# Latent attention of a two-layer decoder: softmax sums formed in all rows of a head, and inverted there

## What is computed

```python
k = jnp.concatenate([k_p, k_r], axis=-1)
q = jnp.concatenate([q_p, q_r], axis=-1)
scores = jnp.einsum('bqhd,bkhd->bhqk', q, k) * scale
scores = jnp.where(causal[None, None], scores, jnp.finfo(scores.dtype).min)
probs = jax.nn.softmax(scores, axis=-1)
out = jnp.einsum('bhqk,bkhd->bqhd', probs, v).reshape(b, s, H)
return out @ o_w
```

## Time and profile before

| | us |
|---|---|
| median of 3 runs | 2243.73 (2242.27 to 2243.81) |
| the profiled execution's own time | 2242.4 |
| its span | 2240.7 |
| PE busy | 2155.5 (96%) |
| PE weight loads busy | 1796.3 (80%) |
| DVE busy | 1315.1 (59%) |
| ACT busy | 1083.3 (48%) |
| POOL busy | 674.5 (30%) |

### The profile page before, as it was taken

One profiled execution on the slowest core, in us unless ns is written; L12 is line 12 of the kernel. 1 busy time (PEld: TensorE's weight loads), 2 busy tenths in 40 slices (PEclk: granted clock), 3 DMA queues, 4 the chain that ended last, 5 costly groups with the idle time before them and its releaser, 6 DMA issues. The chain is left out here.

```text
span 2240.7 us, 43433 instructions
## 1 busy us (share of the span) xinstructions
PE 2155.5 (96%) x18048; PEld 1796.3 (80%) x18048; DVE 1315.1 (59%) x2315; ACT 1083.3 (48%) x1919; POOL 674.5 (30%) x684
## 2 busy tenths in 40 slices
PE   7998899899999999999999999999899999999996
PEld 5766666454589999999999999999777877899996
DVE  7776676689854445444544454444555455767774
ACT  5676533578744444333433343433455554325553
POOL 4111110356412221111111111211354544135663
PEclk9999999999999999999999999999999999999998
DMA  7444302100033232321223123221000000258996
GB/s 282 151 148 140 95 6 114 57 1 1 29 132 123 76 113 95 113 76 64 87 95 113 57 95 120 70 73 57 25 2 2 2 2 30 85 188 265 272 280 105
DMA packets 46931, 215.32 MB, mean 96 GB/s; under 512 B 6160, under 2 KB 6160, under 8 KB 32400
## 3 DMA queue, kind: packets, MB, share of 16 engines
q1 hardware_dynamic: 29968, 139.13, 17.3%
q0 software_dynamic: 16768, 73.41, 11.4%
HBM read 169.00 MB, written 43.52 MB: 95 GB/s over the span
## 5 line engine op out<-in xcount | busy, mean ns | idle before, releaser
L343 POOL TENSOR_TENSOR c_prob<-c_prob,c_inv_mass 128x512 f32<-128x512 f32 x128 | 130.4, 1037 | 353.2 <-DVE c_inv_mass L335 353.2
L325 ACT ACTIVATE c_prob<-abc_banks,c_neg_peak 128x256 f32<-128x256 f32 x256 | 117.7, 472 | 177.6 <-DVE c_neg_peak L317 177.6
L50 PE MATMUL abc_banks<-bc_xt,bc_wq_hi 128*128 128x256 f32 x512 | 147.7, 288 | 0.0
L50 PE MATMUL abc_banks<-c_ctx,c_wk_hi 128*128 128x256 f32 x512 | 146.6, 286 | 0.0
L51 PE MATMUL abc_banks<-bc_xt,bc_wq_hi 128*128 128x256 f32 x512 | 144.9, 283 | 0.0
L52 PE MATMUL abc_banks<-bc_xt,bc_wq_lo 128*128 128x256 f32 x512 | 144.8, 283 | 0.0
L51 PE MATMUL abc_banks<-c_ctx,c_wk_hi 128*128 128x256 f32 x512 | 143.7, 281 | 0.0
L52 PE MATMUL abc_banks<-c_ctx,c_wk_lo 128*128 128x256 f32 x512 | 143.7, 281 | 0.0
L238 PE MATMUL abc_banks<-ab_wq,b_xqt 128*128 128x512 bf16 x512 | 118.7, 383 | 4.2 <-DVE b_h L209 2.2
L2196 DVE TENSOR_TENSOR c_v_lo<-abc_banks,c_v_hi 128x512 fp32r<-128x512 f32 x64 | 44.2, 691 | 133.1 <-ACT c_v_hi L2112 133.1
L1932 POOL DMA_DIRECT2D c_ctx<-kept_scratch x24 | 13.2, 550 | 347.0 <-PE abc_banks L52 347.0
(11 more groups left out here) (590 smaller groups left out, 7223.4 us busy)
## 6 DMA issues: line engine op xcount, KB each, us to landing
x_res<-b_w SPq DMA_DIRECT2D x48, 512.0 KB, 4.7
bc_xt<-kept_scratch POOLq DMA_DIRECT2D x24, 1024.0 KB, 5.1
c_ctx<-kept_scratch POOLq DMA_DIRECT2D x24, 1024.0 KB, 5.2
e_raw<-e_w SPq DMA_DIRECT2D x15, 1536.0 KB
bc_raw<-c_w SPq DMA_DIRECT2D x16, 1024.0 KB, 4.9
h_res<-e_w SPq DMA_DIRECT2D x7, 1536.0 KB
kept_scratch<-bc_xt SPq DMA_DIRECT2D x8, 1024.0 KB, 3.8
kept_scratch<-c_ctx SPq DMA_DIRECT2D x8, 1024.0 KB, 4.0
```

What stands on the lines that cost most here:

```text
L50: pe.matmul(out, lhs[0], rhs[1], start=first, stop=False)
L325: ins = act.activation(self.prob[:, u % 2, j, :], self.s_ps[:, j, :], ACT.Exp, bias=self.neg_peak[:, u % 2, j:j + 1], accum_out=self.mass[ ...
L343: pool.tensor_tensor(part, part, self.inv_mass[:, u % 2, js].unsqueeze(2).to_broadcast([P, 2, SEQ]), ALU.mult).then_inc(self.prob_done, 1)
```

## The change

The sums are formed with a 128x32 matrix of ones, and each group r writes its own 256 columns, so that all 32 rows of a head hold the sum of that head. VectorE takes the reciprocal of all 128x512 into `inv_mass` in SBUF, which has twice the columns, and the divide reads it there. `inverses`, its four products an image and the ring's places n0 and n1 go. ScalarE's `output_high` waits for the new semaphore `divided` instead of the freed bank. GpSimd fills `ones` before the stage begins, and PE and the mask wait for it.

```diff
--- before.py
+++ after.py
@@ -2378,8 +2378,8 @@
         qt_hi, qt_lo = sb("qt_hi", [P, C, SEQ], F32R), sb("qt_lo", [P, C, SEQ], F32R)
         kt_hi, kt_lo = sb("kt_hi", [P, C, SEQ], F32R), sb("kt_lo", [P, C, SEQ], F32R)
         o_hi, o_lo = sb("o_hi", [P, C, SEQ], F32R), sb("o_lo", [P, C, SEQ], F32R)
-        o_f, inv_mass = sb("o_f", [P, 2, SEQ]), sb("inv_mass", [P, SEQ])
-        pick, share, spread_f = picks.pick, picks.share, picks.spread
+        o_f, inv_mass = sb("o_f", [P, 2, SEQ]), sb("inv_mass", [P, 2, SEQ])
+        pick, ones = picks.pick, sb("ones", [P, HD])
         neg_peak = sb("neg_peak", [P, TB, P])
         peak_t = sb("peak_t", [P, SEQ], F32R)
         s_ps = ctx.enter_context(nc.psum_tensor("d_s_ps", [P, 4, 512], F32))
@@ -2409,7 +2409,7 @@
         s_ready, peak_done, st_ready, exp_done, cut_done, w_ready = (
             sem(n) for n in ("s_ready", "peak_done", "st_ready", "exp_done", "cut_done", "w_ready"))
         o_raw_done, o_hi_done, o_lo_done, squared = (sem(n) for n in ("o_raw_done", "o_hi_done", "o_lo_done", "squared"))
-        gain_done = sem("gain_done")
+        gain_done, divided = sem("gain_done"), sem("divided")
         shared_in, small_in, shared_hi_done = sem("shared_in"), sem("small_in"), [sem(f"shared_hi_done{k}") for k in range(2)]
         UP = 2 * (late.raw.shape[1] // 3)
         block = ctx.enter_context(nc.Block())
@@ -2420,8 +2420,8 @@
 
         TURNS = range(-1, BATCH)
         PLACES = (("lq", 1), ("lk", 1), ("mt", 0), ("q0", 1), ("q1", 1), ("k0", 1), ("k1", 1), ("m0", 0), ("v0", 1),
-                  ("qt0", 1), ("qt1", 1), ("n0", 0),
-                  ("kt0", 1), ("kt1", 1), ("m1", 0), ("xt0", 2), ("xt1", 2), ("n1", 0), ("v1", 1), ("o0", 0), ("o1", 0))
+                  ("qt0", 1), ("qt1", 1),
+                  ("kt0", 1), ("kt1", 1), ("m1", 0), ("xt0", 2), ("xt1", 2), ("v1", 1), ("o0", 0), ("o1", 0))
         use_of = {}
         for i in TURNS:
             for name, ahead in PLACES:
@@ -2513,7 +2513,8 @@
 
             pool.memset(mask_f[:, :], 0.0).then_inc(blanked, 1)
             pool.memset(neg_peak[:, :, :], 0.0).then_inc(blanked, 1)
-            pool.wait_ge(blanked, 2)
+            pool.memset(ones[:, :], 1.0).then_inc(blanked, 1)
+            pool.wait_ge(blanked, 3)
             pool.affine_select(out=mask_f[:, :], in_=mask_f[:, :], compare_op=ALU.is_ge, fill=-1e30, base=0,
                                pattern=[[-1, P]], channel_multiplier=1).then_inc(masked, 1)
             pool.wait_ge(rope_in, 16)
@@ -2678,16 +2679,8 @@
                     n = C * i + 2 * h + r
                     for t in range(TB):
                         for j in range(4):
-                            mm = pe.matmul(bank[HD * j:HD * (j + 1), t * P:SEQ], share[:, r, :], prob[:, n % PROBS, j, t * SEQ:SEQ + t * P],
-                                           start=r == 0 and t == 0, stop=r == 1 and t == TB - 1)
-                mm.then_inc(ring_ready, 1)
-
-            def inverses(i, h):
-
-                await_free(pe, f"m{h}", i)
-                bank = claim(f"n{h}", i)
-                for r in range(2):
-                    mm = pe.matmul(bank[:, r * SEQ:(r + 1) * SEQ], spread_f[:, r, :], inv_mass[:, :], start=True, stop=True)
+                            mm = pe.matmul(bank[HD * j:HD * (j + 1), r * SEQ + t * P:(r + 1) * SEQ], ones[:, :],
+                                           prob[:, n % PROBS, j, t * SEQ:SEQ + t * P], start=t == 0, stop=t == TB - 1)
                 mm.then_inc(ring_ready, 1)
 
             def outputs(i, t, half):
@@ -2700,7 +2693,7 @@
                     mm.then_inc(ring_ready, 1)
 
             pe.wait_ge(begun, 1)
-            pe.wait_ge(blanked, 2)
+            pe.wait_ge(blanked, 3)
             for i in TURNS:
                 now, nxt, after = here(i), here(i + 1), here(i + 2)
                 if nxt and i > 0:
@@ -2735,8 +2728,6 @@
                 if nxt:
                     turn_queries(i + 1, 0)
                     turn_queries(i + 1, 1)
-                if now:
-                    inverses(i, 0)
                 if nxt:
                     turn_keys(i + 1, 0)
                     turn_keys(i + 1, 1)
@@ -2757,7 +2748,6 @@
                     turn_inputs(1, 1)
                     keep_busy(pe, o_ps[:, :, :].rearrange("p h q -> p (h q)"), parts["v_u"][0][:, 0:P], parts["v_u"][0], 3)
                 if now:
-                    inverses(i, 1)
                     if i == 0:
                         pe.wait_ge(w_lo_done[OUT], 1)
                         pe.wait_ge(w_lo_done[REST], 1)
@@ -2856,7 +2846,7 @@
             def output_high(i, h):
                 if h == 0 and i > 0:
                     await_ready(act, "o1", i - 1)
-                await_free(act, f"n{h}", i)
+                act.wait_ge(divided, 2 * i + h + 1)
                 act.activation(o_hi[:, 2 * h:2 * h + 2, :], o_f[:, :, :], ACT.Copy).then_inc(o_hi_done, 1)
 
             def square(i, t):
@@ -2973,14 +2963,13 @@
             def invert(i, h):
                 await_ready(dve, f"m{h}", i)
                 if 2 * i + h > 0:
-                    await_ready(dve, f"n{1 - h}", i - 1 + h)
-                dve.reciprocal(inv_mass[:, :], bank_of(f"m{h}", i)[:, 0:SEQ]).then_inc(free_of(f"m{h}", i), 1)
+                    dve.wait_ge(divided, 2 * i + h)
+                dve.reciprocal(inv_mass[:, :, :], bank_of(f"m{h}", i).rearrange("p (r q) -> p r q", r=2)).then_inc(free_of(f"m{h}", i), 1)
 
             def divide(i, h):
-                await_ready(dve, f"n{h}", i)
+                await_free(dve, f"m{h}", i)
                 dve.wait_ge(o_raw_done, 2 * i + h + 1)
-                dve.tensor_tensor(o_f[:, :, :], o_f[:, :, :], bank_of(f"n{h}", i).rearrange("p (r q) -> p r q", r=2),
-                                  ALU.mult).then_inc(free_of(f"n{h}", i), 1)
+                dve.tensor_tensor(o_f[:, :, :], o_f[:, :, :], inv_mass[:, :, :], ALU.mult).then_inc(divided, 1)
 
             def add_to_y(i, t):
                 await_ready(dve, f"o{t}", i)
```

## The result

| us | before | after |
|---|---|---|
| time, median of 8 runs each | 2243.86 (2242.27 to 2249.56) | 2252.34 (2250.47 to 2255.6) |
| the profiled execution's own time | 2242.4 | 2251.46 |
| its span | 2240.7 | 2249.7 |
| PE busy | 2155.5 | 2147.8 |
| DVE busy | 1315.1 | 1341.0 |

The account below looks back on a forecast made before the run. PE was taken as bounding, but held at scores 1 by VectorE's peak behind the second reciprocal. Turns 4.4, last turn 1.0, start 0.1 and end -0.3 gave +5.2 us on the median 2243.73: 2248.9 us, range 2245.2 to 2252.5.

Parts of the forecast that it names:

- the sum: Whole kernel: 4.4 (six turns) + 1.0 (last turn) + 0.1 (stage start) - 0.3 (last image) = +5.2 us.
- list of signs: Wrong if the reciprocal is under 2.6 us, images are no further apart, or the granted clock is below 1.00 within the stage.
- Reciprocal: VectorE's reciprocal, 256 to 512 columns: 1752 to 3352 ns, 1.60 us more, sixteen times.
- First half: Middle image: the query turn waits for the sums' bank, delaying VectorE's chain 0.13 us; PE's saved 1.28 us come to nothing.
- Second half: Middle image: the longer reciprocal delays the peak of scores 0, so scores 1 start 0.73 us later; six turns, 4.4 us.
- Last turn: Image 6 to 7: no input turns ahead, peak close behind the reciprocal; scores 1 at 1878.73 against 1877.69, +1.0 us.
- Rival 2: New PE idle stretches drop the clock to 1.2 GHz, some 1.5 us each turn: +10 more, 2259; chance 0.06.
- End: Last image: divide no longer waits for a slow spreading product; between -1.0 and +0.35 us, taken as -0.3.
- a sentence outside the sum: Last image: the divide's two SBUF operands and GpSimd's selects exclude each other, losing up to 0.3 us more.
- PE's busy time: PE's total busy time was to fall by 16 us or so, as spreading products go.
- Rival 1: Faster, since PE's products count; needs a reciprocal below 2.6 us: -3.5, or -15 without bank waits; chance 0.07.
- rival 3: Partly absorbed: no query-turn wait, earlier peak, or -1.0 usual at the end; +1 to +4, about 2246.5; chance 0.3.

Follow-up runs that it names:

- e5: The changed kernel with six unread products on PE ahead of scores 1 in the turn from image 6 to 7: 2250.75 us, 1.0027 of before.
- e2: The kernel before with each 256-column reciprocal made twice, spreading products kept: 2261.22 us, 1.0093 of before.
- e1: The changed kernel with reciprocals of 256 columns, the first group's inverses serving both groups: 2240.6 us, 0.999 of before.
- e3: The change made for half 0 of the heads only, half 1 as in the kernel before: 2251.61 us, 1.0038 of before.
- e4: The change made for half 1 of the heads only, half 0 as in the kernel before: 2250.38 us, 1.0023 of before.
- e7: The changed kernel with the second reciprocal split around the peak of scores 0, keys' parts ahead of the divide, inputs copied earlier: 2241.01 us, 0.9975 of before.
- e10: The change for half 0 only, half 1 as before, with the keys' parts ahead of the divide: 2240.43 us, 0.9974 of before.
- e9: The kernel before with only the keys' parts moved ahead of the divide, spreading products and n0 kept: 2254.81 us, 1.0046 of before.
- e8: The changed kernel with the keys' parts ahead of the divide and inputs copied earlier, reciprocal whole: 2243.88 us, 0.9991 of before.

## Why the prediction was right

The time came out at 2252.34 against 2248.9, just inside the range of 2245.2 to 2252.5. The mechanism of the turns was right. That the number fell inside was in part luck: the ends that the sum gives itself, +3.6 to +7.5 us, reach only to 2251.2, the 1.6 us that the clock cost had no term in the sum, and the medians lie 2.4 us further apart than the stage explains. By its own list of signs a granted clock below 1.00 within the stage would have made it wrong, and there was one, in the last turn. Step by step:

- **Reciprocal.** 3354 ns for a forecast 3352. The slope between the two widths of the earlier trace rows, 6.25 ns a column, held. By the estimate from the repeat count of 8 in the Trainium skill ("VectorE: DVE Perf Modes", "First, the fixed hardware budget") it would have been 4.3 us. No run agrees with that.
- **First half.** The second query turn started 0.15 after the end of the reciprocal (1722.82 against 1722.67), as forecast, the second low part was 0.15 late, the second reciprocal started 8.54 us after the first instead of 8.40: +0.14 for 0.13. PE stopped at kt1 and the input turns, 0.33 and 0.56, forecast 0.4 and 0.6.
- **Second half.** Scores 1 start 5.07 after the second reciprocal where it was 4.55: +0.52 for 0.60. The timeline of PE:

```profile
1727.48 1.23 PE L2560 MATMUL d_ring<-ident,d_a 128*128 128x128 f32 x8 [0.56 <-DVE d_kt_lo L2953]
...
1732.92 0.39 PE L2635 MATMUL d_s_ps<-d_kt_lo,d_qt_hi 32*128 32x256 f32 x4 [1.30 <-DVE d_neg_peak L2961]
```

  The forecast took 1.83 us for both reductions from the earlier trace rows. Back to back with the reciprocal they took 1731.11 to 1732.87, 1.76 (the first 0.63, not 0.69). So a turn lost 0.66 and not 0.73: 3.9 instead of 4.4.
- **Last turn.** +1.0 was forecast, +2.54 came. This is the step that was wrong: by order it is 0.94, as e5 shows, and the sum had no term for the 1.6 us of the clock there. Rival 2 named the mechanism, priced at 1.5 us a turn and for every turn; it came in one of seven, and cost 1.6. Its two idle stretches are 1.22 and 1.80 us with 3.0 us of work between; in the middle turns the input turns fill most of the first, which is 0.56, and the second is 1.30.
- **End.** -0.3 forecast, -0.4 measured, but the parts were not as told. The bounds of -1.0 to +0.35 were too narrow: e2 aside, the end took 17.94 to 19.93 us, -1.3 to +0.7 by before's 19.27. It matters where in the end the clock is low. e5 has the same instructions there as after and took 19.91 against 18.84. The busy time by stretch, columns as in the earlier trace rows, the first row of after, the second of e5:

```profile
1913.00:1920.00 7.00, 6.04 (x42) 4.28 (x35) 5.84 (x3) 2.40 (x4) 2.63 (x2) 0.51 0.01 2
1917.00:1921.00 4.00, 4.00 (x12) 3.13 (x11) 0.69 (x1) 0.72 (x2) 0.00 (x0) 0.57 0.00 0
```

  In after the output products of half 1 start behind that stretch, at 1921.31; in e5 they start at 1916.67 and run in it. In after, the timeline of the last image (POOL, DVE and PE):

```profile
1910.73 1.23 POOL L2505 TENSOR_SCALAR_AFFINE_SELECT d_prob<-d_prob 128x512 f32<-128x512 f32 x2 [2.27 <-ACT d_prob L2838]
1911.41 1.09 DVE L2972 TENSOR_TENSOR d_o_f<-d_o_f,d_inv_mass 128x512 f32<-128x512 f32 x1
1912.68 2.41 PE L2682 MATMUL d_ring<-d_prob,d_ones 128*32 128x256 f32 x32
1913.31 2.60 POOL L2511 TENSOR_TENSOR d_o_lo<-d_o_f,d_o_hi 128x512 fp32r<-128x512 f32 x1 [1.35 <-ACT d_o_hi L2850]
1915.14 3.36 DVE L2967 RECIPROCAL d_inv_mass<-d_ring 128x512 f32<-128x512 f32 x1 [0.36 <-PE d_ring L2682]
```

  The mass products ran at the lower clock (2.41 us for what takes 1.48), so the second reciprocal had to wait for them. The divide took 1.09 us beside GpSimd's select, and 0.68 or 0.69 in the turns shown: 0.4 more, where up to 0.3 was allowed for in a sentence outside the sum. That agrees with the shared port pair in the Trainium skill, "SBUF — State Buffer" ("Who interferes with whom"): two SBUF operands against a GpSimd instruction that reads SBUF. The other traces bear it out. In before this divide, its second operand in PSUM, ran beside the selects in 0.69; in e1, both operands in SBUF and no select beside it, it took 0.69 too. And in each of e1's six turns the second divide met GpSimd's subtraction for the turned inputs (timelines of POOL and DVE in e1_narrow):

```profile
1688.88 2.37 POOL L2474 TENSOR_TENSOR bc_xt<-d_at_f,bc_xt 128x1024 fp32r<-128x1024 f32 x1 [3.07 <-ACT bc_xt L2797]
1690.27 1.53 DVE L2972 TENSOR_TENSOR d_o_f<-d_o_f,d_inv_mass 128x512 f32<-128x512 f32 x1
```

  It took 1.53 us and ended 0.55 after GpSimd's, as the divide above ended 0.54 after its select (1912.50 against 1911.96). No wait of PE in e1 comes from it.
- **Outside the stage** the profiles differ by 2.9 us, which can't be told from scatter. In the sum: 5.2 forecast for the stage, minus 0.5 in the turns, plus 1.5 in the last turn, minus 0.2 at the stage's two ends gives the measured 6.1, but for rounding.
- **PE's busy time** was to fall by 16 us or so and fell by 7.7. The 2.0 us a turn of the forecast were distances between starts, with a wait of 0.25 in them; in busy time the six turns lost 1.4 each, some 11 in eight images, and the mass products and output products at the lower clock put part of it back.
- **The other rivals.** Rival 1 needed a reciprocal under 2.6 us; at 1.75 (e1) the turn is indeed shorter than before's, by 0.31. Nothing of rival 3 is seen: the query turn waited, and the peak started 0.09 us before the recorded end of the reciprocal, as forecast.

The cause of the loss in the turns, width of the second reciprocal through the peak of scores 0, is shown by e1, e3 and e4. That the savings on PE come to nothing was right only of the step from before to after, where VectorE's chain sets the start of scores 1. Their worth is 0.31 us a turn with the short reciprocal (e1) and 0.88 with the long one (e2).

Not settled: why the clock fell in after's turn 6 to 7. e4 idled 0.48 and 1.78 there and kept 1.00, e5 1.22 and 0.44 and kept it too, after 1.22 and 1.80 and lost it. Each is one profile, and in the last image the same idle time went with different clocks (below), so no rule follows from them.

## What to carry to other kernels

Work taken from the bounding engine comes back only if no other engine's result is then waited for: before moving work to a half-idle engine, look how much idle time that engine has directly ahead of what the first one needs (here 0.61 us, not 19 of 40). A wide operation in an in-order queue should stand behind the short ones that others wait for, and a buffer place that is given up makes room for orders that were closed before (e7 and e10), while the same order with the place kept costs 1.4 us a turn (e9). An idle stretch's price can lie in the clock behind it; compare the same instruction's duration on both sides.

## What the hardware showed that I had not expected

- The reciprocal's time went with its columns over three widths: 252 ns at 16, 1752 at 256, 3354 at 512, 6.25 or 6.26 ns for each column more.
- The same idle time did not always bring the same clock. In the last image PE waited 2.34 us ahead of the spreading product in before, e3 and e10, and that product then took 2.08, 1.13 and 1.41 us.
- GpSimd's subtraction in the last image took 2.60 us in after and 2.85 in before, twice its median, both times beside a VectorE subtraction of two SBUF operands (L2999 in after).
- A divide with both operands in SBUF that met a GpSimd instruction ended 0.54 to 0.55 us after that one, whenever it had started: it took 0.69 us in the turns of after, 0.72 to 0.78 in those of e4, 1.09 in after's last image, 1.53 in the turns of e1 and 1.51 to 1.58 in those of e8. With an operand in PSUM it took 0.69 beside the selects (before, e4 and e9).
